# A two-layer decoder in one program: layer norms' small steps moved to GpSimd, a router by ranks of pairs, a convolution output in halves, and new instruction orders

## The reference

```
x = layernorm(x + mamba(x))            # norm, W_in, causal convolution of 4 taps, silu, selective scan of 16 states over 512 channels, gate, W_out
x = layernorm(x + cosine(x, ctx))      # projected x against projected ctx, each product over both norms
x = layernorm(x + experts(x))          # router: softmax over 4, the 2 best; w * relu(x Wi + lora_e) Wo
x = layernorm(x + attention(x))        # 16 query heads, 4 key heads, rope, low-rank additions folded into the weights
x = layernorm(x + cross(x, ctx))       # norms of both, attention with one head, W_o
x = layernorm(x + recurrent(x))        # gates over the batch as time, then tanh(x Wo + c Uo)

conv = conv_b + sum_k conv_w[k] * xp[.., k:k+L];   xc = silu(conv)
topv, topi = top_k(softmax(x Wg + bg), 2)          # ties go to the lower index
layernorm(x) = (x - mean) / sqrt(var + 1e-5)
```

## Time and profile before

| what | value |
|---|---|
| median of 3 runs | 1385.49 us (1383.58 to 1388.08) |
| the profiled execution, its own time | 1379.84 us |
| its span, first to last instruction | 1377.9 us |
| around the span | 1.9 us |
| mean granted TensorE clock | 0.936 of full speed |
| instructions | 16592 |

### The profile page before, as it was taken

How to read it: one execution, slowest core, us unless ns; L and a number is a source line. 1 busy time by engine, 2 the same in 40 slices (tenths; PEclk the granted TensorE clock), 3 DMA queues, 4 the chain that set the end, 5 groups by cost and what they waited for, 6 DMA issues and landing times.

```text
span 1377.9 us, 16592 instructions
## 1 busy us (share of the span) xinstructions
PE 1160.8 (84%) x5760; PEld 921.4 (67%) x5760; DVE 1056.9 (77%) x1719; ACT 794.5 (58%) x1989; POOL 290.7 (21%) x341
## 2 busy tenths in 40 slices
PE   4697677888899799989998899988998989989852
PEld 2454456666678577866786678867786768868741
DVE  3998899899869797899879897998699763343216
ACT  3433545467658665677567756776477545536521
POOL 0000201222421333232313231324122420010001
PEclk9877999989999899999999999999999999999976
DMA  4612010234424424234414442533343320000301
GB/s 183 242 46 71 7 63 8 77 77 92 101 54 92 89 47 115 58 81 99 110 31 100 86 96 55 110 76 60 92 104 77 50 51 20 1 0 8 121 0 61
DMA packets 55285, 100.27 MB, mean 73 GB/s; under 512 B 5417, under 2 KB 28810, under 8 KB 54562
## 3 DMA queue, kind: packets, MB, share of 16 engines
q0 software_dynamic: 27648, 37.76, 16.8%
q1 hardware_dynamic: 27554, 61.46, 13.8%
HBM read 55.42 MB, written 6.04 MB: 45 GB/s over the span
## 4 chain that ended last, share of the span: by engine, by line
PE 40%; DVE 31%; DMA 9%; ACT 9%; issue 7%; POOL 4%; DVEq 0%; SPq 0%; ACTq 0%; POOLq 0%
PE bank L288 15%; DVE scans L520 10%; DMA scans<-scans 9%; PE bank L1105 4%; DVE scans L516 4%; DVE scans L523 4%; PE bank L1150 3%; PE bank L1123 3%; PE bank L475 2%; DVE nmax L1259 2%; DVE conv L399 2%; PE bank L671 2%; PE bank L883 2%; ACT scans L498 2%; PE bank L889 1%
## 5 line engine op out<-in xcount | busy, mean ns | idle before, releaser
L520 DVE TENSOR_TENSOR_SCAN scans<-scans 128x1024 f32<-128x1024 f32 x128 | 292.3, 2284 | 16.4 <-ACT scans L498 11.9
L498 ACT ACTIVATE scans<-dt,a_neg 128x255 f32<-128x255 f32 x512 | 221.4, 500 | 0.0
L475 PE MATMUL bank<-scans,ident 128*128 128x256 f32 x448 | 138.7, 432 | 49.9 <-DMA scans<-scans 27.0
L1193 ACT ACTIVATE ya<-bank,nmax 128x256 f32<-128x256 f32 x256 | 107.1, 472 | 86.1 <-DVE nmax L1259 86.0
L523 DVE TENSOR_TENSOR scans<-scans,BC 128x1024 f32<-128x1024 f32 x128 | 155.7, 1217 | 1.2
L1259 DVE TENSOR_REDUCE nmax<-bank 128x2 f32<-128x512 f32 x128 | 87.3, 683 | 90.2 <-PE bank L1105 89.1
L516 DVE TENSOR_TENSOR scans<-conv,BC 128x1024 f32<-128x1024 f32 x128 | 155.7, 1216 | 0.1
L552 POOL DMA_DIRECT2D scans<-scans x96 | 84.1, 876 | 289.1 <-DMA scans<-scans 287.8
L475 PEld LDWEIGHTS bank<-scans,ident 128*128 128x128 f32 x448 | 87.8, 210 | 85.5 <-DMA scans<-scans 38.9
L1123 PE MATMUL bank<-v,ya 128*128 128x65 f32 x1024 | 135.5, 278 | 4.4 <-ACT yo L1184 4.4
L1123 PEld LDWEIGHTS bank<-v,ya 128*128 128x128 f32 x1024 | 132.6, 201 | 8.3 <-issue 5.9
(11 more groups left out here) (255 smaller groups left out, 2229.6 us busy)
## 6 DMA issues: line engine op xcount, KB each, us to landing
BC<-xpj_scratch SPq DMA_DIRECT2D x32, 1024.0 KB, 6.1
scans<-scans POOLq DMA_DIRECT2D x96, 256.0 KB, 3.4
scans<-scans POOLq DMA_DIRECT2D x96, 128.0 KB, 2.7
xin<-in_x SPq DMA_DIRECT2D x8, 256.0 KB, 4.3
conv<-in_x SPq DMA_DIRECT2D x8, 256.0 KB, 2.9
out<-scans SPq DMA_DIRECT2D x8, 256.0 KB, 2.7
kept_x<-x SPq DMA_DIRECT2D x7, 256.0 KB, 2.0
kept_w<-wa SPq DMA_DIRECT2D x7, 256.0 KB, 2.0
```

The lines of the kernel that those rows point to most:

```text
L475: last = pe.matmul(sums_of(c), ident[:, :], step_of(b, u)[:, i, :], start=False, stop=(h == UH - 1 and i == SUMMED[b] - 1), skip_group_che ...
L498: ins = act.activation(step[:, j, 1:S], dt[b % 2][:, c, 1:S], ACT.Exp, scale=a_neg[:, c, n:n + 1])
L520: dve.tensor_tensor_scan(flat(H[:, :, :]), flat(H[:, :, :]), flat(dBx), 0.0, ALU.mult, ALU.add).then_inc(s["a_scan"], 1)
L1193: act.activation(pe_[:, h % 2, t, :], YB[h % 2][:, t * S:(t + 1) * S], ACT.Exp, bias=nmax[:, h % 4, t:t + 1]).then_inc(s["t_p"], 1)
```

## The change

1. Layer norms: `stats` ends with `bn_aggr`. `rstd` on POOL does the epsilon and the negated mean first, both on 128x2, then a wait on POOL's own semaphore, then the power and the product. Each norm has its own part of one tile `ln_st`, and one of `ln_small`.
2. Convolution output: two operations of 128x512 in place of four of 128x256, for the tanh on ACT and for the product on DVE. Each takes its input after the same pair of channels as before.
3. Router: each score is compared with each other one (4 x 4), with a table `tie` for equal scores, and the number of those ahead is the rank. Rank 0 is the best, rank 1 the second. One yield fewer on DVE, so its string has 877 letters.
4. `ORDER` is new for all five engines. The number of letters of each stream is the same on PE, ACT, POOL and SP.

```
-        "FFFFSFWWFWFSSYSFYSFYYSYWYSYYSYYSYYSYYSYYSSFSSF...        (pe)
+        "FFFFWWWFFFSSSYYSSYYSYYSWSYFYSYFYYSFYSSFSYYSFYY...
-        "WFWFFFFWFWWWSWSFSSSFSSFSSSSYSSYSSSYSYSSYSYSSYS...        (dve)
+        "WFFFFFWWWWWFWSSFSSSSSSSFSSSSYSYSYSSYSYSFSSYSYS...
...
-        def stats(dve, own, src, st, tag, width=D):
+        def stats(dve, own, src, tag, width=D):
             own.wait()
             for t in range(T):
-                own.did(dve.bn_aggr(ln_mv[tag][:, t, :], ln_sts[st][:, t, :]))
-            own.wait()
-            own.did(dve.tensor_scalar(ln_nm[tag][:, :], ln_mv[tag][:, :, 0], -1.0, None, ALU.mult))
-            return dve.tensor_scalar(ln_var[tag][:, :], ln_mv[tag][:, :, 1], EPS, None, ALU.add)
+                last = dve.bn_aggr(ln_mv[tag][:, t, :], ln_sts[tag][:, t, :])
+                if t < T - 1:
+                    own.did(last)
+            return last
         def rstd(pool, own, tag):
-            own.link(pool.tensor_tensor(ln_rs[tag][:, :], ln_var[tag][:, :], neghalf[:, 0:T], ALU.pow))
-            return pool.tensor_tensor(ln_nb[tag][:, :], ln_nm[tag][:, :], ln_rs[tag][:, :], ALU.mult)
+            own.did(pool.tensor_scalar(ln_rs[tag][:, :], ln_mv[tag][:, :, 1], EPS, None, ALU.add))
+            own.did(pool.tensor_scalar(ln_nb[tag][:, :], ln_mv[tag][:, :, 0], -1.0, None, ALU.mult))
+            own.wait()
+            own.link(pool.tensor_tensor(ln_rs[tag][:, :], ln_rs[tag][:, :], neghalf[:, 0:T], ALU.pow))
+            return pool.tensor_tensor(ln_nb[tag][:, :], ln_nb[tag][:, :], ln_rs[tag][:, :], ALU.mult)
...
-            for e in range(EC):
-                dve.wait_ge(*of("a_xc_tanh", b, e + 1))
-                dve.scalar_tensor_tensor(xc[:, e, :], xc[:, e, :], 1.0, conv[b % 2][:, e, :], ALU.add, ALU.mult).then_inc(s["a_xc"], 1)
+            for j in range(2):
+                dve.wait_ge(*of("a_xc_tanh", b, j + 1))
+                x, y = [flat(a[:, 2 * j:2 * j + 2, :]) for a in (xc, conv[b % 2])]
+                dve.scalar_tensor_tensor(x, x, 1.0, y, ALU.add, ALU.mult).then_inc(s["a_xc"], 1)
...
-            for i, (score, hit, rank, one) in enumerate([(1, 3, 4, 5), (6, 7, 8, 9)]):
-                own.link(dve.tensor_reduce(sc2[:, top, :], sm[:, score, :, :], AX, ALU.max))
-                own.link(dve.tensor_tensor(sm[:, hit, :, :], sm[:, score, :, :], wide(top), ALU.is_equal))
-                own.link(dve.tensor_tensor(sm[:, rank, :, :], sm[:, hit, :, :], tile_of(prio), ALU.mult))
-                own.link(dve.tensor_reduce(sc2[:, best, :], sm[:, rank, :, :], AX, ALU.max))
-                own.link(dve.tensor_tensor(sm[:, one, :, :], sm[:, rank, :, :], wide(best), ALU.is_equal))
...
+            own.link(dve.tensor_tensor(ahead, score.unsqueeze(2).to_broadcast(pairs), score.unsqueeze(3).to_broadcast(pairs), ALU.subtract))
+            own.link(dve.tensor_tensor(ahead, ahead, tie.rearrange("p (e j) -> p e j", e=NE).unsqueeze(1).to_broadcast(pairs), ALU.is_gt))
+            own.link(dve.tensor_reduce(rank, ahead, AX, ALU.add))
+            yield
+            own.did(dve.tensor_scalar(second, rank, 1.0, None, ALU.is_equal))
+            own.did(dve.tensor_scalar(first, rank, 0.0, None, ALU.is_equal))
+            own.did(dve.reciprocal(sc2[:, 2, :], sc2[:, 1, :]))
+            own.wait()
+            own.did(dve.tensor_tensor(sm[:, 7, :, :], second, score, ALU.mult))
+            own.did(dve.tensor_tensor(sm[:, 10, :, :], first, second, ALU.subtract))
+            own.wait()
+            own.did(dve.tensor_reduce(sc2[:, 5, :], sm[:, 7, :, :], AX, ALU.add))
...
```

More of the change, by code:

```diff
@@ L390, in front_dve @@
             dve.wait_ge(*of("a_x", b))
-            stats(dve, own, xin, "f", "a").then_inc(s["a_var"], 1)
+            stats(dve, own, xin, "a").then_inc(s["a_var"], 1)
             yield
@@ L539, in scan_dve @@
             dve.wait_ge(*of("a_res", b))
-            stats(dve, own, res, "s", "a1").then_inc(s["a1_var"], 1)
+            stats(dve, own, res, "a1").then_inc(s["a1_var"], 1)
             yield
@@ L753, in x_dve @@
             dve.wait_ge(*of("b_x2", b))
-            stats(dve, own, xb, "w", "b1").then_inc(s["x_var"], 1)
+            stats(dve, own, xb, "b1").then_inc(s["x_var"], 1)
             yield
@@ L785, in x_dve @@
-            own.link(dve.tensor_tensor(sm[:, 10, :, :], sm[:, 5, :, :], sm[:, 9, :, :], ALU.subtract))
-            for t in range(T):
-                for i, one in enumerate([9, 10]):
-                    own.did(dve.tensor_tensor(low[:, i, t, :].rearrange("p (e r) -> p e r", e=NE),
-                                              low[:, 1, t, :].rearrange("p (e r) -> p e r", e=NE),
-                                              sm[:, one, t, :].unsqueeze(2).to_broadcast([P, NE, RK]), ALU.mult))
+            pairs = [P, T, NE, NE]
@@ new lines, in x_dve @@
+            ahead = sm[:, 2:6, :, :].rearrange("p a t e -> p (a t e)").rearrange("p (t e j) -> p t e j", t=T, e=NE)
+            score, rank, first, second = [sm[:, i, :, :] for i in (1, 6, 8, 9)]
+            own.did(dve.tensor_reduce(sc2[:, 1, :], score, AX, ALU.add))
+            own.link(dve.tensor_tensor(ahead, score.unsqueeze(2).to_broadcast(pairs), score.unsqueeze(3).to_broadcast(pairs), ALU.subtract))
+            own.link(dve.tensor_tensor(ahead, ahead, tie.rearrange("p (e j) -> p e j", e=NE).unsqueeze(1).to_broadcast(pairs), ALU.is_gt))
@@ L791, in x_dve @@
+            own.did(dve.tensor_reduce(sc2[:, 5, :], sm[:, 7, :, :], AX, ALU.add))
+            for i, one in enumerate([9, 10]):
+                own.did(dve.tensor_tensor(low[:, i, :, :].rearrange("p t (e r) -> p t e r", e=NE),
+                                          low[:, 1, :, :].rearrange("p t (e r) -> p t e r", e=NE),
+                                          sm[:, one, :, :].unsqueeze(3).to_broadcast([P, T, NE, RK]), ALU.mult))
             own.wait()
@@ L810, in x_dve @@
             dve.wait_ge(*of("f_res", b))
-            stats(dve, own, x3[b % 2], "w", "f1").then_inc(s["x_var"], 1)
+            stats(dve, own, x3[b % 2], "f1").then_inc(s["x_var"], 1)
             yield
@@ L1003, in z_dve @@
             dve.wait_ge(*of("c_res", b))
-            stats(dve, own, x5, "w", "c1").then_inc(s["z_var"], 1)
+            stats(dve, own, x5, "c1").then_inc(s["z_var"], 1)
             yield
```

113 lines of the change are left out of this document (53 added, 60 removed).

## The result

The changed kernel is slower: 1408.82 us, the median of 4 runs (1401.08 to 1418.34), against 1386.78 for the kernel before, taken with it (4 runs). The ratio is 1.016, with an interval of 1.0087 to 1.0233. The forecast was 1378 with a range of 1362 to 1396, so both its sign and its range are wrong. The profiled execution of the changed kernel is the longest of its four.

The account below looks back on a forecast made before the run. TensorE (40% of the chain) and VectorE (31%) were taken to bound the kernel, each waiting for the other in turn. -10 + 5.1 - 2.5 = -7.4 us gave a median of 1378 us, range 1362 to 1396.

Parts of the forecast that it names:

- The norms, on GpSimd: Epsilon and negated mean moved to GpSimd lengthen each norm by 0.34 us; 15 norms on the chain make +5.1 us.
- The pair costs 0.34, as small neighbours overlap: Epsilon and negated mean on GpSimd overlap as on VectorE; with the wait behind them 0.34 us a norm, bounds 0.34 to 0.48.
- The prediction's other price: By the Trainium skill's half-speed rule for GpSimd, epsilon and negated mean cost 0.68 us, and the chain 11.4 us.
- The scan to wait for is the same one, so contention adds 0: The first new GpSimd operation does the power's wait beside VectorE, cost 0; otherwise 7.4 us for 6 norms.
- Only the 15 norms on the chain count: Of 64 layer norms, 15 powers lie on the chain; the other 49 have slack and cost nothing. All 64 would cost 21.8 us.
- GpSimd gets stuck behind VectorE: Norms' first GpSimd steps meet one more VectorE operation during scans: 23.6 us over 15 norms, net +11.1, 1396.6 us; chance 0.2.
- VectorE's relief, -10: VectorE has 27.1 us less work from norms, router and convolution output; taken as worth 10 us, bounds 0 and 27.1.
- The router: On VectorE, the router falls from 2.96 to 1.75 us a batch, saving 9.7 us of its time in eight batches.
- The convolution's halves: On VectorE, two operations of 128x512 replace four of 128x256, saving 0.8 us of its time and nothing on the path.
- The start, -2.5: Before the first scan: it starts at 41.8 us, 2.9 earlier than before; 2.5 us taken as gain, bounds 0 and 2.9.
- The orders, 0: New order strings of the engines elsewhere than the start: taken as 0, bounds 9.9 us either way.
- laid for other durations: Rival: orders do not fit the chip's durations, TensorE stands early at its sums; +9.9 on -7.4 gives 1388 us; chance 0.2.

Follow-up runs that it names:

- the pair alone: The kernel before with only each layer norm's epsilon and negated mean moved from VectorE to GpSimd: 1404.72 us, ratio 1.0157.
- one more step: The kernel before with each norm's epsilon and negated mean on GpSimd, plus a GpSimd product by 1.0 ahead of the power: 1434.16 us, ratio 1.0345.
- the pair on VectorE: The changed kernel, new orders included, with each norm's epsilon and negated mean back on VectorE: 1382.07 us, ratio 0.9986 to the kernel before.
- the mean only: The kernel before with only each norm's negated mean moved to GpSimd, the epsilon staying on VectorE: 1390.0 us, ratio 1.0044.

## Why the prediction was wrong, point by point

**The step that failed is "The norms, on GpSimd":** +5.1 us, where the pair alone makes +21.7. Three of its choices were wrong.
- *The pair costs 0.34, as small neighbours overlap.* On GpSimd they don't: 0.30 from start to start with or without a wait, 0.61 for the two. Against this stands VectorE's 0.26, no longer ahead of the power. Net the first norm is 0.36 longer, so the number was nearly right by luck: its working was not. The prediction's other price, 0.68 for the pair by half of VectorE's speed, came near the 0.61, but not for its reason: it is for two inputs, and the pair's operations have one. The two operations took 0.23 and 0.22 each, against 0.17 for L269 on VectorE, and what makes the 0.61 is the 0.30 from start to start. Its 11.4 us were too small as well, for the two reasons that follow.
- *The scan to wait for is the same one, so contention adds 0.* This is the wrong end of the bounds. The first step on GpSimd does take the wait that the power had, but the next step then meets VectorE's next operation. The mean grew by 0.77 and not 0.36, and my upper end (7.4 us for 6 norms) had only one such wait in only 6 norms. The mean of 0.77 is also from the traces: a kernel without the contention was not run.
- *Only the 15 norms on the chain count.* The other 49 were said to have slack "until slack is used up", and it was. The upper end that I wrote down, all 64, gave 21.8 with 0.34 each; that this is the 21.7 measured is a coincidence, since a norm grew by 0.77. In the orders of before 0.44 and 0.66 of every added microsecond came out in the time, as if 28 and 42 of 64 norms counted, with wide intervals. The chains of the profiled executions hold 24 powers with the pair alone, 28 in the changed kernel and 32 with one more step. So norms that were not on the chain of before came onto it: their slack was smaller than the latency that they were given.

**The rival "GpSimd gets stuck behind VectorE"** had the place, the mechanism and the sign, and got 0.2. Its price, 1.57 on each of 15 norms = 23.6, is close to the 21.7 measured, but by two errors against each other, which is luck: more norms mattered than it counted, and it put more on each. It came to only 1396.6 because 12.5 us of gains were set against it, and these are not seen in the changed kernel, whose ratio is that of the pair alone.

**VectorE's relief, -10.** The router is right (1.73 against 1.75), but VectorE's busy time fell by 19.3 us and not by 27.1. In the orders of before all of the new code leaves it 1033.2 us, which is 23.7 less; the other 4.4 come back with the new orders, and why isn't settled. The convolution's halves are worth 0.7 us (1048.7 busy without them, 1048.0 with them), as the 0.8 said, though the first two take 1.47 us and not 1.3. Router and convolution free VectorE of 1056.9 - 1048.0 = 8.9 us and gain 0.37% (5.1 us; by the interval 0.8 to 9.4), so the rate of about a third that I used is possible there; the router alone, with 8.2 of these 8.9 us, shows no gain (1.0006), so nothing at all is possible too. What the pair's 15.0 us were worth can't be told apart. The share of an engine in the chain was used as a rate of exchange, and no run here bears that rate out.

**The start, -2.5:** the first scan came at 42.62, 2.07 earlier. Right within 0.5. Whether it saved any time isn't seen beside what the norms cost.

**The orders, 0:** with the old code they cost 0.76%, 10.5 us, by the interval 6 to 15 around my bound of 9.9. With the changed code they cost nothing seen (1.016 against 1.0159), and with the pair on VectorE 0.9986 - 0.9963 = 0.2%, inside the intervals. The term was right for the kernel that it was made for. The rival "laid for other durations" expected longer waits at the sums; they fell to 41.7 us.

Of the signs that I named as wrong, two came: the pair on GpSimd at 0.61 (over 0.5) and GpSimd at 7% of the chain (over 5%). The waits at the sums, 41.7, were 7.9 below those of before, which is some way off the 50 but to the good, and the first scan was not late.

## What to carry to other kernels

Where each engine works through a fixed order, don't count added latency only on the chains that one execution's critical chain holds: others of the same kind come onto it as they grow, here 15 norms before and 24 to 32 after. Test it first by its dose, with one more idle step of the same kind in the unchanged kernel. Don't add small dependent steps on GpSimd beside a VectorE that works on two SBUF operands: there each step waits for one of VectorE's operations, whatever its own size. Before a relief of a busy engine is counted, price the wait that the move adds. And hold a wait against a kernel in the same orders: 97.6 us against 95.6 looks like nothing, and against 69.8 it is the loss.

## What the runs showed of the hardware that I had not expected

- A GpSimd operation that takes 0.22 us alone took 9.54 us beside sixteen scalar products of VectorE back to back, each of 0.69 us with a single SBUF input of 128x1024 (1.22 us for the product of two inputs): it ended at 94.53, behind the last of them. It is one such case in one execution. Beside products and scans GpSimd's operations ended once per VectorE operation.
- Beside 2.27-us scans each dependent GpSimd step ends with a scan: 2.59 us for the power and 1.60 for the small product, 4.37 for both from start to start.
- Two neighbouring GpSimd operations of 0.22 us that don't wait for each other start 0.30 apart, as dependent ones do.
- With the same 5760 products, TensorE was busy 1160.8 us at a mean granted clock of 0.936, 1184.5 at 0.927 and 1186.7 at 0.917 (one more step, idle 246.2 us). Of the 34.3 us between the profiled spans of the last kernel and of the pair alone, 14.7 are idle time and 19.6 are busy time, so idle time is less than half of a loss. That more idle time makes the products slower isn't shown: at the same 0.927 the kernel with the mean only was busy 1174.0, and with nearly the same idle time (231.5) the pair alone 1167.1 at 0.932. These are single executions; by their ratios the two kernels are about 26 us apart.
